# Value sums of four heads at a time, in another place of the attention's pair loop

## What is computed

```python
x = x + attn0(ln(x)); x = x + moe0(ln(x))
x = x + attn1(ln(x)); x = x + moe1(ln(x))
x = x + attn2(ln(x)); x = x + attn3(ln(x)); x = x + moe2(ln(x))
x = x + moe3(ln(x)); x = x + moe4(ln(x))

# attention, per head
attn = softmax(q @ k.T * scale + relative_position_terms)   # attention 3: a causal mask
out = concat_heads(attn @ v) @ proj_w + proj_b
```

## Time and profile before

| | us |
|---|---|
| median of three runs | 495.27 (495.15 to 495.57) |
| the profiled execution, its time | 495.68 |
| the profiled execution, its span | 493.9 |
| PE busy | 461.2 (93% of the span) |
| DVE, ACT, POOL busy | 342.5, 235.5, 172.7 |
| value sums (L808), PE busy | 25.1 |
| scores (L769), transposes of the probabilities (L795), projections (L776) | 44.7, 24.9, 11.0 |

### The profile page before, as it was taken

How to read it: one execution, slowest core, us unless ns; L and a number is a source line. 1 busy time by engine, 2 the same in 40 slices (tenths; PEclk the granted TensorE clock), 3 DMA queues, 4 the chain that set the end, 5 groups by cost and what they waited for, 6 DMA issues and landing times.

```text
span 493.9 us, 8953 instructions
## 1 busy us (share of the span) xinstructions
PE 461.2 (93%) x3088; PEld 379.6 (77%) x3088; DVE 342.5 (69%) x774; ACT 235.5 (48%) x594; POOL 172.7 (35%) x171
## 2 busy tenths in 40 slices
PE   7999899999899899999979898899989999989997
PEld 5746699998555699998645664555679999979997
DVE  3664798996565698997556467441189899878764
ACT  1475356552266485562256237323227645637442
POOL 6044445743044437554025205210045576400000
PEclk9999999999999999999989999999999999999999
DMA  5740046630470045540389400702314655525551
GB/s 151 257 124 1 12 164 199 186 111 3 158 263 1 1 176 168 177 152 0 112 232 275 115 1 0 192 2 83 142 34 146 216 176 171 191 85 172 181 183 35
DMA packets 19363, 62.36 MB, mean 126 GB/s; under 512 B 4041, under 2 KB 6914, under 8 KB 19330
## 3 DMA queue, kind: packets, MB, share of 16 engines
q1 hardware_dynamic: 19330, 61.93, 40.0%
HBM read 59.82 MB, written 2.10 MB: 125 GB/s over the span
## 4 chain that ended last, share of the span: by engine, by line
PE 70%; issue 11%; DVE 8%; POOL 4%; DMA 4%; ACT 2%; SPq 1%; POOLq 0%; DVEq 0%
PE bank L954 25%; PE bank L962 10%; PE bank L974 7%; PE bank L769 7%; PE bank L976 4%; PE bank L795 3%; PE bank L808 3%; POOL probs L425 2%; DMA rel<-rel_scratch 2%; POOL rstd L392 2%; PE bank L752 1%; PE bank L664 1%; DVE nmax L1178 1%; DMA wproj<-in_A_wproj_dram 1%; PE bank L703 1%
## 5 line engine op out<-in xcount | busy, mean ns | idle before, releaser
L954 PE MATMUL bank<-xT_hi,w_hi 128*128 128x256 f32 x408 | 109.2, 289 | 1.6 <-issue 1.6
L1218 DVE TENSOR_TENSOR w_lo<-w,w_hi 128x512 fp32r<-128x512 f32 x102 | 96.9, 988 | 2.1 <-ACT w_hi L555 0.2
L603 ACT ACTIVATE hid<-bank,b 128x256 f32<-128x256 f32 x150 | 62.8, 471 | 68.6 <-PE bank L954 68.4
L954 PE MATMUL bank<-xT_hi,w_lo 128*128 128x256 f32 x408 | 82.0, 282 | 0.0
L954 PEld LDWEIGHTS bank<-xT_hi,w_hi 128*128 128x128 f32 x408 | 77.8, 191 | 3.9 <-issue 3.8
L445 POOL TENSOR_TENSOR w_hl<-w,consts 128x384 fp32r<-128x384 f32 x50 | 52.6, 1052 | 73.3 <-PE bank L976 69.6
L425 POOL TENSOR_TENSOR probs<-probs,rinv 128x512 f32<-128x512 f32 (+1 forms) x44 | 42.8, 991 | 99.1 <-DVE rinv L1182 99.0
L954 PEld LDWEIGHTS bank<-xT_hi,w_lo 128*128 128x128 f32 x408 | 63.4, 191 | 0.0
L447 POOL TENSOR_TENSOR w_hl<-w,w_hl 128x384 fp32r<-128x384 f32 x50 | 58.9, 1179 | 3.9
L962 PE MATMUL bank<-w,hid 128*128 128x192 f32 x308 | 56.4, 327 | 2.3 <-issue 2.3
L555 ACT ACTIVATE w_hi<-w 128x512 fp32r<-128x512 f32 x102 | 58.3, 627 | 0.0
(11 more groups left out here) (162 smaller groups left out, 673.2 us busy)
## 6 DMA issues: line engine op xcount, KB each, us to landing
w<-in_M_w_dram SPq DMA_DIRECT2D x34, 768.0 KB, 5.6
w<-in_M_w_dram SPq DMA_DIRECT2D x33, 576.0 KB, 3.9
w<-in_M_w_dram SPq DMA_DIRECT2D x9, 288.0 KB, 2.8
wqkv<-in_A_wqkv_dram SPq DMA_DIRECT2D x4, 432.0 KB, 7.0
rel_scratch<-relall SPq DMA_DIRECT2D x4, 372.0 KB, 2.3
wproj<-in_A_wproj_dram SPq DMA_DIRECT2D x4, 288.0 KB, 7.7
wqkv<-in_M_w_dram SPq DMA_DIRECT2D x2, 576.0 KB, 21.5
kT<-in_M_w_dram SPq DMA_DIRECT2D x2, 576.0 KB, 6.9
```

Of the source, the lines that this page charges most:

```text
L603: ins = act.activation(hid[:, 2 * b + c, :], bank[B_H[b]][:, c * T:(c + 1) * T], FUNC[cfg["act"]], bias=b1[:, kb, bass.ds(at, 1)])
L954: ins = pe.matmul(bank[B_H[b]][:, c2 * T:(c2 + 1) * T], w, xs, start=(q == 0), stop=(q == 4))
L1218: dve.tensor_tensor(w1_cols(w1_lo, b), w1_cols(w1[s], b), w1_cols(w1_hi, b).bitcast(F32), ALU.subtract)\
```

## The change

values_summed takes a group of four heads instead of a pair. It waits until the transposed probabilities of both pairs of the group have been copied to pT, then runs, for each kt, the products of the four heads one after the other, and signals once per group instead of once per pair. It is called ahead of the transposes of the even pairs 2 and 4 (after the scores, where there are any), and for the last group at the end. The first two projections are moved behind the last transposes. The order on PE:

```diff
 def outputs(g):
-    act.wait_ge(o_psum, n * PAIRS + 2 * (g + 1))
+    act.wait_ge(o_psum, n * GROUPS + g + 1)
     act.activation(oT[:, g, :], bank[B_O[g]][:, 0:T], ACT.Copy).then_inc(o_ready, 1)
...
-def values_summed(p):
-    pe.wait_ge(pT_act, n * PAIRS + p + 1)
-    pe.wait_ge(pT_dve, n * PAIRS + p + 1)
-    if p == 4:
+def values_summed(g):
+    pe.wait_ge(pT_act, n * PAIRS + 2 * g + 2)
+    pe.wait_ge(pT_dve, n * PAIRS + 2 * g + 2)
+    if g == 2:
         pe.wait_ge(o_ready, GROUPS * n + 1)
     for kt in range(TT):
-        for h in range(2):
-            row = 32 * ((2 * p + h) % 4)
-            first_q = kt * P if n == 3 else 0
-            ins = pe.matmul(bank[B_O[p // 2]][row:row + 32, first_q:T], v_st[:, kt, 2 * p + h, :],
-                            pT[:, p % 2, kt, h, first_q:T], start=(kt == 0), stop=(kt == TT - 1),
-                            skip_group_check=(n == 3))
+        first_q = kt * P if n == 3 else 0
+        for head in range(4):
+            ins = pe.matmul(bank[B_O[g]][32 * head:32 * (head + 1), first_q:T], v_st[:, kt, 4 * g + head, :],
+                            pT[:, head // 2, kt, head % 2, first_q:T], start=(kt == 0),
+                            stop=(kt == TT - 1), skip_group_check=(n == 3))
     ins.then_inc(o_psum, 1)
...
 for p in range(PAIRS):
...
     if p + 2 < PAIRS:
         pe.wait_ge(p_ready, (TT * PAIRS - 1) * n + TT * p + 1)
         scores(p + 2)
+    if p % 2 == 0:
+        values_summed(p // 2 - 1)
     probs_transposed(p)
-    values_summed(p - 1)
-    if p + 2 >= PAIRS:
-        project(p + 2 - PAIRS)
-values_summed(PAIRS - 1)
+for g in range(GROUPS - 1):
+    project(g)
+values_summed(GROUPS - 1)
 project(GROUPS - 1)
```

## The result

The changed kernel is slower, and by far more than I forecast: 506.99 us in the median of four runs (502.17 to 508.56) against 495.33 for the kernel before, a ratio of 1.0219 (95% interval 1.0147 to 1.0290; the ratios in this document can differ by up to 0.2% from the quotient of the two medians beside them, here 1.0235). I had said 497.4, within 495.6 to 501.8. On another chip it measured 505.76 against 495.58, again 1.0219 (1.0154 to 1.0284). Of the four runs there the highest, 509.25, is over 1.5% above the lowest and counts as slow; without it the median is 504.90. The profiled execution has a span of 506.1 us, 12.2 more than before.

A forecast was written before the change was run, and what follows sets the result against it. TensorE (PE) was taken to set the pace; 3.2 us of work removed per attention returned as waits, losing 3 x 0.52 + 0.49, about 2.1 us. Forecast 497.4 us, own range 496.6 to 498.3, wider range 495.6 to 501.8.

The forecast's parts named there:

- the walk: Block-by-block timing of the attentions' pair loops after the change: 0.52 us lost in each of three, 0.49 in attention 3.
- J(2): Last projection of an attention on PE; forecast 17.13 us after T(1) instead of 16.61 in attentions 0 to 2.
- T(1): Transposes of pair 1 on PE, from which the changed stretch of each attention is timed.
- G(1): Second four-head value-sum block on PE; forecast to stand idle 2.08 us, waiting for DVE's copy of pair 3.
- T(5): Transposes of pair 5 on PE; forecast to wait 0.95 us for the copy of pair 4.
- T(2): Transposes of pair 2 on PE; forecast 0.88 us late because the first four-head block now stands ahead of them.
- S(4): Scores of pair 4 on PE, now right after T(1); forecast to wait for POOL's normalised pair 2, gaining only 0.2 us.
- four beats: Forecast length of a four-head value-sum block, all heads side by side: 0.99 us, the same as for two heads.
- rival 1: Clock falls in PE's new loop gaps, some 1.2 us: 498.6 us with one, 502.2 with four; chance 0.2.
- Rival 2: The old clock fall at 249.58, before attention 2, costing 1.5 us, may not come again: 495.9 us; chance 0.12.
- Rivals 3 and 4: Four-head blocks: 3, eight beats, 507.1 us, chance 0.08; 4, packing at the skill page's rate, 499.8 to 500.3, chance 0.06.
- Rival 5: DVE's copy of pair 3 isn't behind pair 5's row maxima, so G(1) starts earlier: 493.4 us; chance 0.04.

The follow-up runs named there:

- f1_again: The changed kernel run again unaltered, beside its variants on another chip: 505.76 us, single times 499.45 to 509.25.
- e1_fill: The changed kernel with useless warm-up products in three PE gaps (one ahead of S(4), four ahead of G(1), two ahead of T(5)): 497.79 us.
- e3_dve: The changed kernel with DVE's copy of pair 3 moved ahead of the row maxima of pair 5, gaps filled with warm-up products: 496.43 us.
- f3_fill_t5: The changed kernel with two warm-up products ahead of T(5) alone, none ahead of G(1): 502.14 us, ratio 1.0121.
- f4_8beats: As e1_fill, but the last two heads of a group write to the first two's places, so at most two run side by side: 506.25 us.
- e4_slots: Four-head groups kept but placed behind the transposes, pT given a third part, first projection ahead of the fifth transposes, one warm-up product: 490.62 us, ratio 0.9888.
- e2_pairs: As e1_fill, but in each group the products of heads 0 and 1 are issued ahead of those of heads 2 and 3: 497.39 us.
- f2_fill_g1: The changed kernel with four warm-up products ahead of G(1) alone: 497.98 us, ratio 1.0032.

## Why the prediction was wrong

**Right, nearly to the digit: the walk.** At full clock (f1_again, attentions 1 to 3) J(2) comes 17.13 us after T(1) (walk: 50.91 - 33.78 = 17.13), and 15.73 in attention 3 (walk: 15.80). That the first agrees to the digit is partly luck: G(1) comes 0.09 us and T(5) 0.14 later than in the walk, and the blocks behind them make up for it. T(2) is late by 0.89 (0.88 said), S(4) starts 1.74 after T(1) (1.74), the stand ahead of G(1) is 2.0 (2.08), the one ahead of T(5) 0.83 (0.95; T(5) itself 13.26 after T(1), 13.12 said). G has four beats, 1.07 us for 16 records. PE works 13.10 us in such a loop instead of 16.13, 3.0 less. The loss of 2.1 us is what the loops show without falls, 2.0; that e1_fill's whole time, 497.79, lies so near the forecast is chance, since the kernel before took 496.61 beside it. The cause named, DVE's copy behind the row maxima, is shown by e3_dve.

**Wrong: the sum counts falls of the clock in the loops as nothing.** They stood in rival 1 alone, at "some 1.2 us" each, one per loop at most, with a chance of 0.2 for all of it. In the first profile all four loops had one, and they cost 8.4 of the 12.2 us. Measured are 1.46 for a fall of 3.4 us and 2.87 for one of 6.8, which I hadn't considered at all. And the chance was put at a fifth on the argument that the gap of 2.08 us "has G close behind". That was the wrong way to read the one row I had: 2.09 us of idle had let the clock fall in the kernel before, and I was about to make four such gaps (2.60 us long in attention 3), with the stand ahead of T(5) behind each; f3_fill_t5 shows that this second stand counts too. A fall in every loop at 1.46 us gives 497.4 + 5.8 = 503.2; the measured median is 9.6 above the walk's sum, because some falls last 6.8 us and others come outside the loops. The range's top of 501.8 lay below even my own price for four falls, 502.2.

**Wrong in size: the old fall.** Rival 2 took the runs of before being alike as a sign that the fall at 249.58 always comes. Beside the experiments the same kernel took 493.0 to 501.0 us in 62 runs on three chips. The times go with the mean granted clock: 493.0 to 494.2 in the six runs at 1.000, 498.2 to 499.4 in the eleven at 0.990, 501.0 in the two at 0.986. Its falls change from one execution to the next, and the first four just happened to agree. Rival 2's event did come, none at 249.6, but other falls at 12.0 and 295.3 more than took its gain back. A difference below one per cent needs many runs here.

**Rivals 3 and 4** are excluded for this kernel: eight beats would be 1.92 us (f4_8beats), the block took 1.07. The 3.07 times that the Trainium skill gives for four row tiles ("TensorE: Matmul & The Clock Gate", Measured speedup) would have made it an estimated 1.3 us; the trace has 1.06 us for two heads' products and 1.07 for four heads', so here the second pair of heads costs no measurable time. **Rival 5** would have needed what e3_dve did by hand; even that ends level with the kernel before (0.9994).

The remark of the Trainium skill ("TensorE: Matmul & The Clock Gate", Part 4) that transposes don't count as busy for the clock in the same way was not tested by itself. Loops with three T and no long stand kept 2.4 GHz (e1_fill, e4_slots); the falls inside the loops came where long idle and transposes stood together.

## What to carry to other kernels

Where an engine is nearly always busy and a change takes work from it, look for the block that is moved ahead of another engine's feed. Here 3.0 us of work saved per attention came back as waits and 0.5 more, because T(2) was made 0.9 us late and the removed blocks had covered waits. Count a stand of some 2 us on PE as two costs, its length and a granted clock that may fall behind it, here 1.5 us or more each time. Useless products that fit into the stand cost nothing here: 17.14 us with them, 17.13 without. And before pricing a gain by one profile, know how much the program's own executions differ.

## What the runs showed of the hardware that I had not expected

- Four heads' products that write different places of 32 columns ran side by side in both orders tried: the block took 1.07 us with the four heads one after the other and 1.08 us in e2_pairs, where two of them come behind both key tiles of the other two. With two places it took 1.92. Whether PE or the compiler brings them together was not settled.
- The clock fell by stretches of 3.4 us, or two of them in a row, 6.8 us, and was back at full speed between. Which loop is hit differs between executions of one program: in the first profile of the changed kernel all four loops were, in the second only that of attention 0.
- With the gap of 2.0 us (2.6 in attention 3) ahead of G(1) filled to under half a microsecond (at most 1.1 in attention 3), no loop of the five profiled kernels that had it so (e1_fill, e2_pairs, e3_dve, f2_fill_g1, f4_8beats) showed a fall.
